# Joint causal masks and masked maxima in an attention stage, with the next group's scores spread over six steps instead of five

## The reference, cut to what matters

```python
k, q, v = proj(W_key), proj(W_query), proj(W_value)           # (b, 16 heads, 512, 16)
scores = jnp.einsum('bhqd,bhkd->bhqk', q, k) * hd ** (-0.5)
scores = jnp.where(causal, scores, -jnp.inf)
weight = jax.nn.softmax(scores, axis=-1)
out = jnp.einsum('bhqk,bhkd->bhqd', weight, v)                # then W_proj
...
w = softmax(-dists / t); top 2 of 32 prototypes; y = A[idx] (B[idx] x) + bias[idx]
x = x + s * silu(g)                                           # s: attention, g: experts
```

## Time and profile before

| | us |
|---|---|
| median of 3 runs | 1098.41 (1097.14 to 1102.90) |
| the profiled execution | 1094.69 |
| its span, first to last instruction | 1092.9 |
| stages 1, 2, 3 of one entry and 0 of the next | 19.63, 18.23, 21.80, 21.46 |

### The profile page before, as it was taken

How to read it: one execution, slowest core, us unless ns; L and a number is a source line. 1 busy time by engine, 2 the same in 40 slices (tenths; PEclk the granted TensorE clock), 3 DMA queues, 4 the chain that set the end, 5 groups by cost and what they waited for, 6 DMA issues and landing times.

```text
span 1092.9 us, 20884 instructions
## 1 busy us (share of the span) xinstructions
PE 1016.9 (93%) x6846; PEld 701.1 (64%) x6846; DVE 501.8 (46%) x1139; ACT 518.9 (47%) x1379; POOL 192.9 (18%) x184
## 2 busy tenths in 40 slices
PE   3789999999999967989999999999999999999986
PEld 2457777777777754556666666666666656656663
DVE  4522112121121264547457467467467467466451
ACT  2424444444444524256456456456456456454443
POOL 3201001010010052131312312312313213200000
PEclk9889999999999987899999999999999999999999
DMA  6541101011012024435135145245235244224110
GB/s 198 193 136 39 48 29 58 29 39 47 29 58 106 31 86 123 70 98 146 43 131 137 45 137 127 53 135 120 65 133 111 68 140 101 68 73 112 31 40 20
DMA packets 63760, 94.22 MB, mean 86 GB/s; under 512 B 11760, under 2 KB 49136, under 8 KB 63728
## 3 DMA queue, kind: packets, MB, share of 16 engines
q1 hardware_dynamic: 57456, 89.36, 29.0%
q10 hardware_dynamic: 6272, 4.46, 1.3%
HBM read 59.94 MB, written 33.59 MB: 86 GB/s over the span
## 4 chain that ended last, share of the span: by engine, by line
PE 81%; DVE 7%; issue 3%; ACT 3%; DMA 2%; ACTq 1%; SPq 1%; POOL 0%; DVEq 0%; POOLq 0%
PE PS L768 25%; PE PS L972 7%; PE PS L874 6%; PE PS L926 6%; PE PS L907 5%; PE PS L941 5%; PE PS L840 4%; PE PS L755 4%; PE PS L819 3%; PE PS L1003 3%; DVE nm L1622 3%; PE PS L861 2%; PE PS L928 2%; PE PS L943 2%; ACTq L1236 1%
## 5 line engine op out<-in xcount | busy, mean ns | idle before, releaser
L768 PE MATMUL PS<-arena 128*128 128x256 f32 x1024 | 312.1, 421 | 0.0
L1622 DVE TENSOR_REDUCE nm<-PS 128x1 f32<-128x512 f32 (+3 forms) x352 | 207.2, 636 | 89.6 <-PE PS L928 89.5
L1293 ACT ACTIVATE arena<-PS 128x512 f32<-128x512 f32 x256 | 152.2, 600 | 168.2 <-PE PS L943 167.0
L1160 ACT ACTIVATE arena<-PS 64x8 f32<-64x8 f32 x512 | 88.5, 173 | 184.4 <-PE PS L755 180.7
L755 PEld LDWEIGHTS PS<-arena 128*72 128x72 f32 x1024 | 129.9, 141 | 68.1 <-ACT arena L1160 4.6
L768 PEld LDWEIGHTS PS<-arena 128*128 128x128 f32 x1024 | 155.5, 192 | 0.0
L941 PE MATMUL PS<-Q,K 98*128 98x512 bf16 (+3 forms) x512 | 130.9, 301 | 7.6 <-ACT arena L1293 5.6
L1478 DVE SCALAR_TENSOR_TENSOR arena<-arena 128x512 f32<-128x512 f32 x16 | 11.1, 694 | 265.7 <-ACT arena L1171 265.7
L926 PE MATMUL PS<-K,Q 96*128 96x256 bf16 (+3 forms) x512 | 121.1, 304 | 4.4 <-DMA K<-qk_d 2.5
L755 PE MATMUL PS<-arena 128*72 128x8 f32 x1024 | 121.3, 191 | 0.0
L928 PE MATMUL PS<-negmask,identb 128*128 128x128 bf16 x512 | 96.2, 222 | 0.0
(11 more groups left out here) (172 smaller groups left out, 1324.3 us busy)
## 6 DMA issues: line engine op xcount, KB each, us to landing
qk_d<-QB SPq DMA_DIRECT2D x24, 512.0 KB, 3.0
X<-in_L_attn_x SPq DMA_DIRECT2D x12, 512.0 KB, 3.5
Q<-qk_d SPq DMA_DIRECT2D x32, 192.0 KB, 4.0
K<-qk_d SPq DMA_DIRECT2D x32, 192.0 KB, 4.3
arena<-xt_d SPq DMA_DIRECT2D x16, 256.0 KB, 3.2
gt_d<-arena SPq DMA_DIRECT2D x16, 256.0 KB, 2.5
wx_d<-arena SPq DMA_DIRECT2D x16, 256.0 KB, 2.0
XT<-xt_d SPq DMA_DIRECT2D x8, 512.0 KB, 4.5
```

Source lines behind the costliest of these rows:

```text
L768: mm = pe.matmul(o, lhs, rhs, start=first, stop=last)
L1293: s_.activation(PR[:, g % 2, j, at:at + T], PS[:, bank, :], ACT.Exp, scale=SCORE_SCALE).then_inc(t_e.sem, 1)
L1622: v_.tensor_reduce(nm[:, g, h:h + n, i], PS[:, u % 3, 0:n * (i + 1) * P].rearrange("p (n w) -> p n w", n=n), AX.X, ALU.max, negate=True).t ...
```

## The change

The masks: one-head units (0 to 7) get no mask matmul at all. VectorE adds a mask from SBUF (`rowmask`, 512 wide, zeros but for the last 128 columns) while it takes the maximum, with one `tensor_tensor_reduce` that writes the sum back to PSUM and the maximum to `nm`; a one-column memset stands ahead of it. Units 8 to 10 get one joint mask matmul instead of two or four, and so do the turned tiles that share a bank. The maxima are no longer negated by VectorE but one step on, by ScalarE and VectorE in `maxima_high` and `maxima_low`.

The order: `STEP_OF` spreads the eleven units over steps 0 to 5 instead of 0 to 4, `maxima_turn` moves from step 6 to step 7 on TensorE, `maxima_high` from behind `exp` of step 6 to behind that of step 7, and the DMAs of `take_maxima` from behind `exp` of step 7 to behind that of step 8. The side tables are otherwise the same, VectorE's among them.

```diff
-STEP_OF = (0, 0, 0, 1, 1, 2, 2, 3, 3, 4, 4)
+STEP_OF = (0, 0, 1, 1, 2, 2, 3, 3, 4, 5, 5)
...
                 for e in range(n):
-                    pe.matmul(PS[:, bank, e * w:(e + 1) * w], Q6[0:KS, g * GH + h + e, i * P:(i + 1) * P],
-                              K6[0:KS, g * GH + h + e, 0:w], start=True, stop=False)
-                    mm = pe.matmul(PS[:, bank, (e + 1) * w - P:(e + 1) * w], identb[:, :], negmask[:, :],
+                    mm = pe.matmul(PS[:, bank, e * w:(e + 1) * w], Q6[0:KS, g * GH + h + e, i * P:(i + 1) * P],
+                                   K6[0:KS, g * GH + h + e, 0:w], start=(e == 0), stop=(n == 1))
+                if n > 1:
+                    mm = pe.matmul(PS[:, bank, 0:n * w].rearrange("p (n w) -> p n w", n=n)[:, :, w - P:],
+                                   identb[:, :], rowmask[:, T - P:].unsqueeze(1).to_broadcast([P, n, P]),
                                    start=False, stop=True)
...
-                        if k == 6:
+                        if k == 7:
                             maxima_turn(*nxt)
...
-                side = {6: [lambda: maxima_high(b, 1)], 7: [lambda: take_maxima(b, 1)]}
+                side = {7: [lambda: maxima_high(b, 1)], 8: [lambda: take_maxima(b, 1)]}
...
-                    side[6] = [lambda: maxima_high(b + 1, 0)]
-                    side[7] = [lambda: take_maxima(b + 1, 0)]
+                    side[7] = [lambda: maxima_high(b + 1, 0)]
+                    side[8] = [lambda: take_maxima(b + 1, 0)]
...
-                v_.tensor_reduce(nm[:, g, h:h + n, i],
-                                 PS[:, u % 3, 0:n * (i + 1) * P].rearrange("p (n w) -> p n w", n=n), AX.X, ALU.max,
-                                 negate=True).then_inc(m_r.sem, 1)
+                w = (i + 1) * P
+                if n > 1:
+                    v_.tensor_reduce(nm[:, g, h:h + n, i], PS[:, u % 3, 0:n * w].rearrange("p (n w) -> p n w", n=n),
+                                     AX.X, ALU.max).then_inc(m_r.sem, 1)
+                else:
+                    v_.memset(begun[:, u:u + 1], 0.0)
+                    v_.tensor_tensor_reduce(out=PS[:, u % 3, 0:w], in0=PS[:, u % 3, 0:w], in1=rowmask[:, T - w:],
+                                            scale=1.0, scalar=-BIG, op0=ALU.add, op1=ALU.max,
+                                            accum_out=nm[:, g, h, i:i + 1]).then_inc(m_r.sem, 1)
```

More of the change, by code:

```diff
@@ L533, in _ @@
             g_.memset(ident[:, :], 0.0).then_inc(const, 1)
-            g_.memset(negmask[:, :], 0.0).then_inc(const, 1)
+            g_.memset(rowmask[:, :], 0.0).then_inc(const, 1)
             g_.memset(negmask_t[:, :], 0.0).then_inc(const, 1)
@@ L546, in _ @@
                              pattern=[[-1, P]], channel_multiplier=1).then_inc(const, 1)
-            g_.affine_select(out=negmask[:, :], in_=negmask[:, :], compare_op=ALU.is_ge, fill=-BIG, base=0,
+            g_.affine_select(out=rowmask[:, T - P:], in_=rowmask[:, T - P:], compare_op=ALU.is_ge, fill=-BIG, base=0,
                              pattern=[[-1, P]], channel_multiplier=1).then_inc(const, 1)
@@ L936, in maxima_turn, with turned_tile @@
                              ).then_inc(m_t.sem, 1)
-            def turned_tile(b, h, kt, bank, at):
+            def turned_tile(h, kt, bank, at, first):
                 w = T - kt * P
                 pe.matmul(PS[:, bank, at:at + w], K6[0:KM, h, kt * P:(kt + 1) * P],
-                          Q6[0:KM, h, kt * P:T], start=True, stop=False)
-                return pe.matmul(PS[:, bank, at:at + P], identb[:, :], negmask_t[:, :],
-                                 start=False, stop=True)
+                          Q6[0:KM, h, kt * P:T], start=first, stop=False)
             def turned(b, g, k):
@@ L951, in turned @@
                 h, bank = g * GH + k // 5 * 2 + k % 5 // 2, 3 + k % 2
+                blocks = PS[:, bank, :].rearrange("p (a q) -> p a q", q=P)
                 if k % 5 == 4:
-                    turned_tile(b, h - 2, 2, bank, 0)
-                    mm = turned_tile(b, h - 1, 2, bank, 2 * P)
+                    turned_tile(h - 2, 2, bank, 0, True)
+                    turned_tile(h - 1, 2, bank, 2 * P, False)
+                    edge = blocks[:, 0:4:2, :]
                 elif k % 5 % 2 == 0:
-                    mm = turned_tile(b, h, 0, bank, 0)
-                else:
-                    turned_tile(b, h, 1, bank, 0)
-                    mm = turned_tile(b, h, 3, bank, 3 * P)
-                mm.then_inc(t_mm.sem, 1)
+                    turned_tile(h, 0, bank, 0, True)
+                    edge = blocks[:, 0:1, :]
+                else:
+                    turned_tile(h, 1, bank, 0, True)
+                    turned_tile(h, 3, bank, 3 * P, False)
+                    edge = blocks[:, 0:4:3, :]
+                n = edge.shape[1]
+                pe.matmul(edge, identb[:, :], negmask_t[:, :].unsqueeze(1).to_broadcast([P, n, P]),
+                          start=False, stop=True).then_inc(t_mm.sem, 1)
             def values(b, g):
@@ L1333, in stage1 @@
             def stage1(b, more, first=False):
-                side = {1: [lambda: take_values(b, 0)], 6: [lambda: maxima_high(b, 2)], 7: [lambda: take_maxima(b, 2)]}
+                side = {1: [lambda: take_values(b, 0)], 7: [lambda: maxima_high(b, 2)], 8: [lambda: take_maxima(b, 2)]}
                 if more:
@@ L1340, in stage1 @@
                     side[7].append(lambda: take_query_key(b + 1, 2))
-                    side[8] = [lambda: middle(b + 1, 0), lambda: take_query_key(b + 1, 3)]
+                    side[8] += [lambda: middle(b + 1, 0), lambda: take_query_key(b + 1, 3)]
                     side[9] = [lambda: middle(b + 1, 1)]
@@ L1348, in stage2 @@
                 side = {1: [lambda: take_values(b, 1)], 5: [lambda: expert_gate(b, 0)],
-                        6: [lambda: maxima_high(b, 3)], 7: [lambda: take_maxima(b, 3)], 8: [],
+                        7: [lambda: maxima_high(b, 3)], 8: [lambda: take_maxima(b, 3)],
                         9: [lambda: expert_gate(b, 1)]}
```

11 lines of the change are left out of this document (6 added, 5 removed).

## The result

The changed kernel is slower, by more than the forecast said. Three executions took 1175.52, 1183.81 and 1186.95 us, beside 1099.63 for the kernel before on the same chip: 1.0758 times as long, with a 95% interval of 1.0721 to 1.0794. (A fourth execution was disturbed, took 1545.93 and stands outside the ratio; with it the median is 1185.38.) The forecast was 1158, its wide range 1132 to 1192. So the direction and the range held, and the forecast's own range, up to 1180, did not.

What follows compares the result with a forecast made beforehand. TensorE, busy 93% of the span, was taken to set the time. Seven entries (55 us at 7.9 each) plus 6 gave +61 on 1094.7, and 3.7 for the median: 1158 us, own range 1135 to 1180, wide range 1132 to 1192.

Steps and rivals of the forecast that it cites:

- masks, a stage: On TensorE's path, fewer mask matmuls save 0.51 us a stage, 16 us for 32 stages.
- masked maximum of 512, pitch: On VectorE, a maximum with the mask added takes 0.75 instead of 0.60 us, 1.2 us a stage.
- wait ahead of `low_rank(1)`: Stage 3, step 4: TensorE waits 1.5 us for `weigh(0)`, which stands behind the maximum of unit 8.
- `low_rank_turn(3)`, behind its step's mask: Stage 3, step 7: it starts 2.0 us after that mask instead of 0.62, waiting for `weigh(3)` behind `maxima_low`; +1.4.
- next stage behind `low_rank_turn(3)`: End of stage 3: the later DMA makes the next stage begin 3.4 us after it instead of 2.10; +1.3.
- wait ahead of `heads_turn`: Stage 0: TensorE waits 2.0 us for `divide`, behind units 6 and 7 on VectorE.
- first stage and the ends: The first stage, the eleven units ahead of the stages and the last entry's stages 1 and 2 add 6 us.
- Rival D: TensorE's clock falls while it idles in stage 3, adding 4 us per entry: 1186 us; chance 7%.
- rival C: The masked maximum on VectorE costs 1.2 us a unit, about 5 us more an entry: 1195 us; chance 8%.
- E: Joint masks run at half rate on TensorE, +35 us: 1193 us; chance 3%.
- A: The waits are filled after all and only 16 us of TensorE mask work goes: 1082 us, faster; chance 3%.
- B: Only the later DMA issue in stages 3, 2 and 1 costs, 19 against 16 us: 1101, no change; chance 4%.

Runs made afterwards that it cites:

- e8: Kernel before with the changed masks in the old order, plus VectorE's inner loop written out so it never jumps back: 1087.24 us, ratio 0.9889.
- e9: Changed kernel with fourteen idle products on TensorE in stage 3's waits, including the one for the DMA: 1170.30 us, ratio 1.0642 to the kernel before.
- e12: Changed kernel with VectorE's inner loop written out, nothing else: 1175.21 us, ratio 1.0693 to the kernel before.
- e2: Kernel before with the new order alone (six steps, later maxima turn and DMAs), all masks as before: 1196.05 us, ratio 1.0872.
- e3: Changed kernel with units still over six steps, but the maxima's turn back in step 6 and DMAs behind step 7: 1149.31 us, ratio 1.0473 to before.
- e4: Changed kernel with units back in five steps, but the maxima's turn still in step 7 and DMAs one step later: 1145.99 us, ratio 1.0430 to before.
- e6: Changed kernel with VectorE's weighings one or two units earlier and `weigh(3)` ahead of `maxima_low`: 1141.16 us, ratio 1.0392 to the kernel before.
- e1: Changed kernel with the old order restored, so only the masks differ from the kernel before: 1099.22 us, ratio 0.9995 to before.

## Why the prediction was right, and where it fell short

Its terms, against the profiled execution:

| step of the prediction | forecast | measured |
|---|---|---|
| masks, a stage | -0.51 | -0.43 (e8: 79.4 for 81.1 us in four) |
| masked maximum of 512, pitch | 0.75 | 0.63 |
| wait ahead of `low_rank(1)` | 1.5 | 1.38 |
| wait ahead of `low_rank(2)` | 1.5 | 1.53 |
| `low_rank_turn(3)`, behind its step's mask | 2.0 | 2.25 (903.74 to 905.99) |
| next stage behind `low_rank_turn(3)` | 3.4 | 3.50 (905.99 to 909.49) |
| stage 3 | +5.4 | +5.4 |
| wait ahead of `heads_turn` | 2.0 | 1.55 |
| stage 0 | +0.8 | +0.3 at whole clock (e9), +2.4 as it ran |
| DMA's wait at the end of stage 1 | 0.5 | 0.54 |
| stage 1 | +0.8 | +0.9 without the loop's turn (e12), +2.6 with it |
| stage 2 | +0.9 | +0.8 |
| first stage and the ends | +6 | +3.6 |

**The steps on the order held.** They were three latencies (0.25 from matmul to VectorE, 0.69 for a 512-column operation, 0.05 back) put on the new order, with the work in between taken off, and they reproduce each wait of stage 3 to a quarter of a microsecond. e2, e3, e4 and e6 put them on the order alone: each part of it costs what it does at the places named.

**The clock was the first thing missed.** From the start of stage 1 in the first entry to the same point in the last, seven entries took 565.6 us before and 642.8 after. That is +77, where the forecast had 55. Stage 0 at the lower clock was about 2.1 us too long in six entries, and up to 1.9 in the last, 14 in all; two of the stages 2 also lost 1.0 each. Rival D had the mechanism, at 7% and at another place (inside stage 3, 4 us an entry). The step that failed is the reading of the earlier trace rows: one wait of 2.18 us under a whole clock was taken as evidence for a stage that has four waits of 1.4 to 1.9 us, two of them close together. e3 against e4 shows that it was those two, and e6 that one of them alone mostly leaves the clock whole.

**VectorE's code was the second.** The masks' step priced the masked maximum in time and not in instructions. The four stages 1 at the turn of the loop took 1.6 to 1.7 us more than the others, 6.6 in all, and e12 takes just these away. No rival had it. In the old order it is the difference between no change (e1) and 1.1% faster (e8).

**The masked maximum** was dearer in the forecast than on the chip, by 0.12 us a unit; rival C is dead, and so is E: a joint mask of 256 columns gives way to the next matmul after 0.11 us (896.24 to 896.35), twice the 0.06 of one of 128. `heads_turn` was 0.45 us too high, about as much as stage 0's own sum was (0.5 an entry); that the one is the other's cause wasn't tried. A and B fell with stage 3's length.

**From the terms to 1158.** Without the lower clock and the turns, some 54.5 of the +77 us are left, and the forecast had 55. That is in part luck: an ordinary entry's four stages come to 7.4 us and not 7.9, and the last entry's stage 3 grew by 7.6 us (20.26 to 27.82) and not by 5.4. The prediction's last sum is also short by about 1.5 us: 1094.7, 61 and 3.7 make 1159.4, not 1158. e9 takes 13.5 us off 1183.8 and e12 8.6, the latter not clear of noise; with both off, if they add, 1161.7 is left (an estimate), 4 us from the forecast. The median also stands 8.3 us above the profiled execution, not 3.7: the other two executions had a mean clock of 0.948 where the profiled one had 0.953. So the terms on the order were sound, and what was missed came on top of them in the same direction, which is why the result lies above the forecast's own range.

What stays open: how the clock falls are spread over single executions, which a profile of one cannot tell, and whether it is the length of VectorE's loop body alone, somewhere between 237 and 269 recorded instructions, or also its place in the code that makes the turn wait.

## What to carry to other kernels

When work is moved a step later on one engine, the tables of the engines that answer it must move too. Read for each consumer what then stands between the producer and it: the latency of the chain less the work in between is the wait, and it could be worked out to a quarter of a microsecond in stage 3, and to 0.45 in stage 0. Count instructions as well as time wherever a loop body grows; cheap extra instructions can make each turn wait for code, and the idle time shows as "issue" at the head of the body, with more packets on the instruction queue. And when a change adds several waits on TensorE close together, price the clock too: it makes the work behind the last wait dearer, in a stage that the change may not touch.
